# Projections of a cross-attention kernel from float32r halves to scaled float16 halves, with the key scale moved

## What is computed

```python
Q = (layernorm(x) @ Wq.T + bq).reshape(bs, sl, 16, 32)
K = (ctx @ Wk.T + bk).reshape(bs, sl, 16, 32)
V = (ctx @ Wv.T + bv).reshape(bs, sl, 16, 32)
score  = einsum('bshd,bsgd->bshg', Q, K)      # over the 16 heads of one token
weight = softmax(score)
attn   = einsum('bshg,bsgd->bshd', weight, V)
x = x + attn @ Wo.T + bo
x = x + ffn(layernorm(x))   # shared gated FFN + top 2 of 8 experts
```

## Time and profile before

| | before |
|---|---|
| median of 3 runs | 1497.16 us (1495.56 to 1502.17) |
| the profiled execution's own time | 1501.36 us |
| its span, first to last instruction | 1499.6 us |
| busy: PE, PE weight loads, DVE | 1404.5, 1070.5, 910.6 us |
| busy: ACT, POOL | 647.0, 504.6 us |
| mean granted TensorE clock | 0.979 |

### The profile page before, as it was taken

One profiled execution on the slowest core, in us unless ns is written; L12 is line 12 of the kernel. 1 busy time (PEld: TensorE's weight loads), 2 busy tenths in 40 slices (PEclk: granted clock), 3 DMA queues, 4 the chain that ended last, 5 costly groups with the idle time before them and its releaser, 6 DMA issues.

```text
span 1499.6 us, 32986 instructions
## 1 busy us (share of the span) xinstructions
PE 1404.5 (94%) x10371; PEld 1070.5 (71%) x10388; DVE 910.6 (61%) x1984; ACT 647.0 (43%) x1500; POOL 504.6 (34%) x607
## 2 busy tenths in 40 slices
PE   4899999999999998789999899999999999999997
PEld 4788888888888887557666666666666666657675
DVE  5888888888888887848764542222222222224565
ACT  6355556666666666622253433333333333332121
POOL 4444444444444442201566201111111111104554
PEclk9899999999999999799999999999999999999998
DMA  5556667666666775658655342222222222227996
GB/s 194 135 126 176 176 175 176 175 175 175 179 183 179 190 204 150 219 207 307 88 53 78 74 133 86 84 84 79 82 84 84 77 85 83 84 70 222 306 323 196
DMA packets 261893, 223.20 MB, mean 149 GB/s; under 512 B 182997, under 2 KB 191261, under 8 KB 261486
## 3 DMA queue, kind: packets, MB, share of 16 engines
q1 hardware_dynamic: 241224, 178.62, 42.6%
q0 software_dynamic: 12880, 35.47, 8.3%
q10 hardware_dynamic: 7734, 8.40, 1.9%
HBM read 129.30 MB, written 67.96 MB: 132 GB/s over the span
## 4 chain that ended last, share of the span: by engine, by line
PE 78%; DVE 8%; DMA 7%; ACT 3%; issue 2%; SPq 1%; POOL 0%; another core or an unknown queue 0%; ACTq 0%; DVEq 0%; POOLq 0%
PE psum_b L716 41%; PE psum_a L716 30%; PE psum_b L1032 2%; DMA base<-x_rows 2%; DMA base_rows<-base 2%; PE psum_a L813 2%; PE psum_b L1054 2%; ACT spread_t L1100 1%; DVE d_m L1716 1%; SPq L487 1%; DMA out_rows<-wgu_in 1%; PE psum_b L742 1%; DMA heads<-in_wk_t 1%; DVE base L1711 1%; ACT z_parts L1136 1%
## 5 line engine op out<-in xcount | busy, mean ns | idle before, releaser
L716 PE MATMUL psum_a<-wgu,zg_t 128*128 x1704 | 266.1, 313 | 1.9 <-DVE zg_t L1813 1.7
L1952 POOL TENSOR_TENSOR spread<-pr,own 128x512 f32<-128x512 f32 x128 | 136.7, 1099 | 303.2 <-DVE pr L1468 292.0
L716 PEld LDWEIGHTS psum_a<-wgu,zg_t 128*128 128x128 f16 x1704 | 165.3, 98 | 89.2 <-issue 10.1
L2026 POOL DMA_INDIRECT zg<-z_rows,gather_ix x71 | 67.2, 946 | 414.9 <-DVE gather_ix L1809 407.6
L716 PE MATMUL psum_a<-zt_in,wsgu 128*128 128x256 f16 x1536 | 177.0, 279 | 10.5 <-DMA base<-x_rows 7.5
L716 PEld LDWEIGHTS psum_a<-zt_in,wsgu 128*128 128x128 f16 x1536 | 152.1, 100 | 37.7 <-DMA base<-x_rows 9.0
L1818 DVE SCALAR_TENSOR_TENSOR silu<-psum_a,w_scale,silu 128x352 f32<-128x352 f32 x71 | 41.4, 584 | 192.0 <-ACT silu L1307 192.0
L716 PE MATMUL psum_b<-wdn,act_t 128*128 (+1 forms) x639 | 149.7, 379 | 1.6 <-DVE act_t L1825 1.6
L716 PE MATMUL psum_b<-wsdn,sh_t 128*128 128x512 f16 (+1 forms) x576 | 133.7, 386 | 16.8 <-DVE sh_t L1697 16.2
L1307 ACT ACTIVATE silu<-psum_a,w_scale 128x352 f32<-128x352 f32 x71 | 39.3, 553 | 200.8 <-PE psum_a L716 200.8
L716 PEld LDWEIGHTS psum_b<-wsdn,sh_t 128*128 128x128 f16 (+1 forms) x576 | 54.4, 99 | 90.4 <-issue 17.8
(11 more groups left out here) (245 smaller groups left out, 2510.7 us busy)
## 6 DMA issues: line engine op xcount, KB each, us to landing
expert_rows<-y_sb SPq DMA_DIRECT2D x71, 256.0 KB, 2.0
k_st<-k_parts SPq DMA_DIRECT2D x192, 64.0 KB, 2.1
q_st<-q_parts SPq DMA_DIRECT2D x180, 64.0 KB, 2.1
wgu_in<-in_wgu_t SPq DMA_DIRECT2D x8, 1408.0 KB, 17.4
x_sb<-in_x SPq DMA_DIRECT2D x16, 512.0 KB, 4.1
cx_in<-in_ctx_t SPq DMA_DIRECT2D x16, 512.0 KB, 7.0
x_res<-in_x SPq DMA_DIRECT2D x16, 512.0 KB, 5.5
value_rows<-heads SPq DMA_DIRECT2D x16, 512.0 KB, 7.0
```

What stands on the lines that cost most here:

```text
L716: return nc.tensor.matmul(o, l, r, start=start, stop=stop)
L1952: G.tensor_tensor(spread[:, u * UG:(u + 1) * UG, :].rearrange("p r (g t) -> p r g t", t=GT), pr[:, s, u * UG:(u + 1) * UG, :].unsqueeze(3) ...
L2026: pool.indirect_dma_start(out=zg[:, b, :], out_offset=None, in_=z_d[:, :], in_offset=bass.IndirectOffsetOnAxis(ap=gather_ix[:, b:b + 1], a ...
```

## The change

K, Q and V take float16 parts under power-of-two scales: 2^11 for normalised x, a scale per block for the context (`k_next`, columns 4 and 5), a scale per weight (`w_power`). V is unscaled when it is read. The sizes of `wq`, `wk`, `wv`, `xn_t`, `cx_t` halve. Since the context's scale must be known before it is split, the context block is loaded a second time, one block earlier, into `cx_w` (`load_cw`), reduced there three blocks ahead, and the seven instructions of the key scale now run behind `normalise_out`; `take_key_scale` at their old place is two instructions. POOL's `split_context` waits for it and has one more instruction over 128 x 1024. In the prologue three rounds of limits take the place of one, and the low parts of wk, wq, wv are all made by DVE. Cut to its core:

```diff
+        cx_w = sb("cx_w", [P, KC, BT], F32, early)
+        cx_t = sb("cx_t", [P, 2, KC, BT], F16, early)
+        wq, wk, wv: [P, 2, KC, D], F16;  xn_t: F16
+        LIMITS = [(0, 3), (3, 5), (5, 6)]
@@ sync, prologue
             load_w(wk_in, wk_t, wk_loaded)
+            load_cw(1)
             load_w(wq_in, wq_t, wq_loaded)
...
-            sp.wait_ge(cx_weighed, 1)
+            sp.wait_ge(cx_weighed, 2)
             load_cx(1)
+            load_cw(2)
             move_keys(-1)
             sp.wait_ge(xn_ready, 2 * SUB)
             load_x(2)
+            sp.wait_ge(cx_weighed, 3)
+            load_cw(3)
             store_values(-1)
@@ sync, body
                 if ahead:
                     store_values(i)
+                if ahead3 and ahead4:
+                    sp.wait_ge(cx_weighed, i + 4)
+                    load_cw(i + 4)
                 if ahead3:
-                    sp.wait_ge(cx_weighed, i + 3)
                     sp.wait_ge(cx_split, i + 3)
                     load_cx(i + 3)
@@ tensor, prologue
             turn_x(-1)
-            pe.wait_ge(wk_split, 1)
+            turn_limits(0)               # 3 transposes
+            pe.wait_ge(wk_split, 2)
             project_k(-1, range(KC))
-            (4 transposes of limit_rep)
+            turn_limits(1)               # 2
+            turn_limits(2)               # 1
             pe.wait_ge(wq_split, 1)
             project_q(-1, range(KC))
             pe.wait_ge(wv_split, 1)
             project_v(-1)
@@ scalar, prologue
-            weights_high(wk ...); x_out(-1); weights_high(wq ...); weights_high(wv ...)
             (two mask copies)
-            weights_high(wo, wo_in, wo_loaded, 32)
+            x_out(-1)
+            scaled_high(0, wk, ..., slice(0, KC // 2))
+            scaled_high(0, wk, ..., slice(KC // 2, KC))
+            scaled_high(1, wq, ..., slice(0, KC))
             keys_out(-1, 0); keys_out(-1, 1); queries_out(-1, 0); queries_out(-1, 1)
+            scaled_high(2, wv, ..., slice(0, KC))
             act.wait_ge(q_low, 2)
             (12 DMAs that move the queries)
+            weights_high(wo, wo_in, wo_loaded, 32)
@@ vector
+            def take_key_scale():
+                link(V.tensor_scalar(k_bound[:, 3:4], k_scale[:, 2:3], q_scale[:, 3:4], None, ALU.mult))
+                V.tensor_copy(k_scale[:, 2:10 + KC], k_next[:, 2:10 + KC]).then_inc(k_scaled, 1)
@@ vector, values_out and x_low
-                    V.tensor_tensor(v_rows[:, s], bank_ap(f"V{s}"), bv_rep[:, :], ALU.add)
+                    V.scalar_tensor_tensor(v_rows[:, s], bank, k_scale[:, 8:9], bv_rep, mult, add)
@@ vector, body
                 own_scores(i, 0, range(2))
-                next_key_scale(i - 1)
+                take_key_scale()
...
                 if behind:
                     normalise_out(i)
+                if ahead2:
+                    next_key_scale(i - 1)   # 7 instructions, then c_scaled
...
-                if ahead2:
-                    weigh_context(i + 2)
+                if ahead3:
+                    weigh_context(i + 3)    # reads cx_w
                 if ahead:
                     spread_context()
@@ vector, prologue
+            weigh_context(0)
+            dve.wait_ge(wk_loaded, 16);  largest_of(0, wk_in)
+            dve.wait_ge(bias_loaded, 64); largest_of(1, bias_col[:, 1, :])
+            weigh_context(1); max;  spread_limits(0)
+            key_scales()                     # limits_out(0), w_scaled, key scale, c_scaled
+            k_scale <- k_next
+            scaled_low(0, ...) for two halves of wk -> wk_split
             x_low(-1)
+            largest_of(3, bias), largest_of(4, wq_in); spread_limits(1)
+            query_scales()                   # limits_out(1), w_scaled
+            largest_of(5, wv_in); spread_limits(2)
+            scaled_low(1, ..., wq) -> wq_split
+            value_scales()                   # limits_out(2), w_scaled
             own, strip_sum
             low_heads K0, K1; weigh_context(2); spread_context; low_heads Q0, Q1
+            scaled_low(2, ..., wv) -> wv_split
             x_stats(1); normalise_x(1); values_out(-1); split_bias()
@@ gpsimd, split_context
+                pool.wait_ge(c_scaled, i if not isinstance(i, int) else max(i, 1))
+                link(G.tensor_scalar(cx_in[:, :, :], cx_in[:, :, :], k_next[:, 5:6], None, ALU.mult))
                 link(G.tensor_copy(cx_t[:, HI], cx_in[:, :, :]))
-                low(G, cx_t[:, LO], cx_in[:, :, :], cx_t[:, HI]).then_inc(cx_split, 1)
+                G.tensor_tensor(cx_t[:, LO], cx_in, cx_t[:, HI], ALU.subtract).then_inc(cx_split, 1)
@@ gpsimd, prologue
-            weights_low(2, wq, wq_in, wq_split)
-            weights_low(3, wv, wv_in, wv_split)
...
-            weights_low(4, wo, wo_in, wo_split)
+            weights_low(5, wo, wo_in, wo_split)
```

More of the change, by code:

```diff
@@ L193, in build @@
         bv_rep = sb("bv_rep", [P, D], F32, one)
[L194 to L196 removed]
+        limits = sb("limits", [P, 6], F32, one)
+        q_scale = sb("q_scale", [P, 5 + KC], F32, one)
+        k_bound = sb("k_bound", [P, 4], F32, one)
+        w_power = sb("w_power", [P, 8], F32, one)
+        k_next, k_scale = (sb(n, [P, 10 + KC], F32, one) for n in ("k_next", "k_scale"))
         own = sb("own", [P, GT], F32, one)
@@ L573, in load_piece, with body @@
                     sp.dma_start(weigh_in[0:FS - 5 * P, 2 * D:PIECE], wsdn_t[5 * P:FS]).then_inc(piece_loaded, 16)
-            def body(i, behind, ahead, ahead3, rows_from=None):
+            def body(i, behind, ahead, ahead3, rows_from=None, ahead4=True):
                 fetch_values(i)
@@ L895, in _, with turn_limits @@
             turn_x(-1)
-            pe.wait_ge(wk_split, 1)
+            def turn_limits(phase):
+                pe.wait_ge(limits_ready, phase + 1)
+                for n in range(*LIMITS[phase]):
+                    at = phase * BANK + (n - LIMITS[phase][0]) * P
+                    last = nc.tensor.transpose(psum_a[:, at:at + P], limit_rep[:, n, :], ident[:, :])
+                last.then_inc(limits_turned, 1)
+            turn_limits(0)
+            pe.wait_ge(wk_split, 2)
             project_k(-1, range(KC))
[L898 to L901, removed]
+            turn_limits(1)
+            turn_limits(2)
             pe.wait_ge(wq_split, 1)
@@ L1408, in weigh_context @@
                 dve.sem_inc(cx_weighed, 1)
             def spread_context():
[L1411 to L1423, removed]
+                V.tensor_copy(c_rep[:, :], k_bound[:, 2:3].broadcast_to([P, P])).then_inc(c_rep_ready, 1)
@@ new lines, in limits_out, with weight_scale @@
+            def limits_out(phase):
+                first, end = LIMITS[phase]
+                dve.wait_ge(limits_turned, phase + 1)
+                link(V.tensor_reduce(out=limits[:, first:end], in_=psum_a[:, phase * BANK:phase * BANK + (end - first) * P].rearrange("p (n c) -> p n c", c=P),
+                                     axis=X, op=ALU.max))
+            def weight_scale(n, limit):
+                power, up = (w_power[:, at:at + 1].bitcast(U32) for at in (n, 3 + n))
+                link(V.tensor_scalar(power, limits[:, limit:limit + 1].bitcast(U32), EXPONENT, None, ALU.bitwise_and))
+                link(V.tensor_scalar(power, power, float(SMALLEST << 23), None, ALU.max))
+                link(V.tensor_scalar(up, power, -1.0, float((2 * 127 + W_EXP) << 23), ALU.mult, ALU.add))
+                dve.sem_inc(w_scaled, 1)
@@ L1539, in weigh_piece, with body @@
                     V.tensor_reduce(out=seen[:, bass.ds(i, 1)], in_=weigh_in[:, 0:n], axis=X, op=ALU.max, apply_absolute_value=True).then_inc(weighed, 1)
-            def body(i, behind, ahead, ahead2, weighs=0):
+            def body(i, behind, ahead, ahead2, weighs=0, ahead3=True):
                 bound_out(i - 1)
@@ L1635, in _, with largest_of, spread_limits @@
-            V.tensor_copy(limit_rep, limits[:, :].unsqueeze(2).broadcast_to([P, 4, P])).then_inc(limits_ready, 1)
+            def largest_of(n, values):
+                mark(V.tensor_reduce(out=limits[:, n:n + 1], in_=values, axis=X, op=ALU.max, apply_absolute_value=True))
+            def spread_limits(phase):
+                first, end = LIMITS[phase]
+                own_.wait()
+                V.tensor_copy(limit_rep[:, first:end], limits[:, first:end].unsqueeze(2).broadcast_to([P, end - first, P])).then_inc(limits_ready, 1)
@@ new lines, in _ @@
+            dve.wait_ge(wk_loaded, 16)
+            largest_of(0, wk_in.rearrange("p c n -> p (c n)"))
+            dve.wait_ge(bias_loaded, 16 * 4)
+            largest_of(1, bias_col[:, 1, :])
+            own_.wait()
+            weigh_context(1)
+            link(V.tensor_tensor(limits[:, 2:3], limits[:, 2:3], k_bound[:, 2:3], ALU.max))
+            spread_limits(0)
+            key_scales()
+            V.tensor_copy(k_scale[:, 2:10 + KC], k_next[:, 2:10 + KC]).then_inc(k_scaled, 1)
+            for half in range(2):
```

(1 more changed line is left out.)

149 lines of the change are left out of this document (97 added, 52 removed).

## The result

The changed kernel takes **1517.84 us** (median of 4 runs, 1516.06 to 1520.99) against 1497.63 (1495.56 to 1502.17): a ratio of **1.0151**, interval 1.0112 to 1.0190. Its span is 1519.3 us, 19.7 more than before. The range and the sign of the prediction held. Two of its steps did not: what sets a pass, and what POOL's new instruction costs. Runs on other chips are given as a ratio to the kernel before, measured on the same chip.

A forecast was written before the change was run, and what follows sets the result against it. The passes looked bound by PE, but SP's 36.64 us loop was taken to bind. Prologue 19.4 - 1.4 - 1.2 from the passes = +16.8 us, 1514 on the median; forecast 1513, range 1501 to 1523.

The forecast's parts named there:

- The loop gives 2.6 us: Passes: total gain 2.6 us, from 1.4 of slack by pass 11 and 1.2 in passes 12 to 14.
- SP stays at 36.64 and binds: Passes: SP's queue and DMA loop keeps its 36.64 us period, so PE ends up waiting for query parts.
- DVE's 35.9: Passes: DVE's loop after the change, about 35.9 us, summed from z-to-end 8.1 and end-to-z 27.8.
- The end-to-z term: Passes, DVE from a pass's end to the second z: 27.8 us, 28.9 before.
- The z-to-end term: Passes, DVE from z to the pass's end: 8.1 us, 7.5 before, with `c_rep` ending with POOL's longer split.
- POOL's multiply, 1.1 us: POOL's added multiply over 128 x 1024 in the context split: 1.1 us, between 1.04 and 2.37.
- Matmuls: Passes, PE: 96 float16 matmuls of 256 columns save 0.9 us a pass; V nothing, bounds -0.2 to +0.2.
- Prologue: Start of the kernel: K at 25.5, Q 40.7, V 54.3, pass 0's bound at 76.6 against 56.97, +19.6 us.
- SP does not bind: Rival, passes: the engines' 35.9 us hold for 14 passes, -5.6 instead of -2.6 us; chance 0.12.
- The passes lengthen: Rival, passes: POOL's multiply at the two-operand price or SP's fetch behind the second context load, 1520 to 1528; chance 0.15.
- Float16 gives PE nothing: Rival, PE's matmuls: the 111 ns is from another tile mix, 1516; chance 0.07.
- Faster: Rival, prologue: added steps hide under existing waits, body 0 begins within 4 us of 56.97, total 1488; chance 0.06.

The follow-up runs named there:

- run 8: Kernel before with unscaled float16 tiles, POOL's parts behind z, bias split early, and DVE's expert-weight search cut to 512 columns: 1482.95 us.
- run 1: Changed kernel with DVE's search for the expert weights' scale cut to 512 columns from 1536 or 1408: ratio 1.0133.
- run 3: Changed kernel without POOL's multiply, so the context is not scaled: ratio 1.0171.
- run 4: Kernel before with the tiles of wq, wk, wv, xn_t and cx_t in float16, unscaled, same order of work: 1530.03 us, ratio 1.0195.
- run 10: Changed kernel with the prologue reordered: query weight's limits turned ahead of the first K, wv's parts made ahead of the query parts: ratio 1.0075.
- run 9: As run 8, and SP moves only two of the three key parts in the passes: 1471.62 us.
- run 5: As run 4, and in the passes POOL begins the next slab's parts only when both halves of z are written: ratio 0.9948.
- 11: As run 5, with the bias split early and POOL's second spread of a pass waiting for both halves of the next xn: ratio 0.9909.
- run 6: Kernel before with the ten instructions that split the output bias moved in front of the second slab's statistics: ratio 0.9971.

## Why the prediction was right, and where it was wrong

- **"The loop gives 2.6 us": wrong, and by the step "SP stays at 36.64 and binds".** The passes lost 1.2 us (+21.6 at the end of pass 0, +22.8 at that of pass 14). DVE's loop was put at 35.9 and is 36.65. SP's period before the change was read rightly: when DVE is relieved, SP's slack runs out and passes go to 36.5 (run 8). But in the kernel after, SP's lead was never used up. The forecast of a pass, 36.6, was right for a wrong reason, and one of the prediction's own signs of being wrong came: passes 8 to 11 took 36.51, less than SP's loop of 36.64. The second context load, put at 0, seems to cost SP 0.3 us a pass: its x loads are 36.90 apart in run 1, where it binds, and were 36.64 without that load. No run takes the load out.
- **DVE's 35.9 is 36.5 by the same two stretches, and failed in both.** The end-to-z term, 27.8, is 29.1: "-1.0 us ahead of z" did not arrive. `x_low` waits 0.82 us for ACT, as the text allowed for. The other loss I did not see: xn takes 0.88 us a half in the mean instead of 0.57 (the two groups below). All of it is in the second half, 1.37 us for 0.54, because the spread on POOL no longer waits for PE and starts under it. From the end of a pass to the second z it is 29.1 us (400.08 to about 429.2), as before (376.54 to 405.69). The z-to-end term, 8.1, is 7.4: `c_rep` was to end with POOL's subtraction, and ended with its cast. These two errors, 1.3 too little and 0.7 too much, partly cancel.

```profile
L1390 DVE TENSOR_SCALAR xn<-x_sb,mv,rstd 128x512 f32<-128x512 f32 x32 | 18.0, 565 | 3.9 <-POOL rstd L1908 3.0
```

That was the kernel before; the kernel after:

```profile
L1419 DVE TENSOR_SCALAR xn<-x_sb,mv,rstd 128x512 f32<-128x512 f32 x32 | 28.1, 877 | 4.0 <-POOL rstd L2004 3.0
```

- **POOL's multiply, 1.1 us: 2.86 to 3.91.** The upper bound, 2.37, was too low as well: here the form with one tensor and a scalar column is dearer than the form with two tensors. In the passes it hardly matters (0.15 us, run 3): POOL is then at its cast when `c_rep` is due and holds it until 435.6, where before it was at its subtraction; in the prologue it is on the path.
- **Matmuls: K and Q as said** (24 K in 2.64 us from start to start, 110 ns). V was counted at 0, bounds 0.2; it gives 5.72 - 5.34 = 0.4 us. Of the 2.0 us by which V's end moved against z in run 4, these are 0.4; the rest is its earlier start against z. A sum can be right to 0.4 us and still miss what a sooner end sets free.
- **Prologue: +19.6 said, +20.9 found.** K 25.5 (28.27), Q 40.7 (43.25), V 54.3 (56.75), bound 76.6 (77.83). K was 2.8 late: 1.4 because the scales were ready at 20.8 and not at 19.4, and 1.4 because POOL's three instructions behind them took 7.3 us (3.91, 1.04 and 2.12, and the gaps), where 6.1 had been allowed with the conflict. wk's two low halves took 3.26 instead of 2.56 beside the multiply, but ended at 24.03 and were not on the path. Q and V are 2.5 late as well, the bound 1.2. Q at the lower clock was right: 7.1 said, 7.20 found, with 0.50 granted from 42 to 46 us, behind a pause of PE. I costed the limits turned behind K, and wv's parts behind the queries, as facts of the change; run 10 shows that this order, not the work, is 13 of the 20.9 us.
- **The rivals.** "SP does not bind" was right of SP, but the passes did not come to the engines' 35.9. "The passes lengthen" named the right engine with the wrong consequence: the multiply came above its price, the passes lengthened by 0.2 to 0.3 us, not 0.6. "Float16 gives PE nothing" is out (run 9). "Faster" is out: pass 0's bound came 20.9 us late, where it needed under 5.
- **The end, and luck.** The sum gave +16.8 us; at the end of pass 14 it was +22.8. The 6 us are 2.2 up to the end of pass 0 (21.6 against 19.4) and 3.8 in passes 1 to 14, where a gain of 2.6 was said and a loss of 1.2 came. At the end of the run +19.7 was left. That difference is less than the part behind pass 14 varies, and no run tells whether it is the change's: by it the number looks closer than the working was.

The Trainium skill, "SBUF — State Buffer" (the shared port pair), says that a VectorE instruction in a two-port mode, or one with two SBUF inputs beside a GpSimd instruction that reads SBUF, shares a pair of ports with GpSimd: whichever starts first has them for its whole length, and the other blocks. For `c_rep` the trace agrees: its copy, 0.23 us alone, ends 0.1 us after POOL's cast. It shows the same in two places where I did not apply it: z at 425.23 and 426.45, whose halves ended 0.28 us after POOL's cast and its subtraction (428.51), and the second half of xn, which ended 0.28 us after POOL's first spread instruction (in the kernel after, the two starts lie within 0.04 us, too close to say which was first). Runs 5 and 11 remove these overlaps, and z goes from 1.42 to 0.54 us a half, xn from 0.84 to 0.57. For the splits of the prologue it held only in part. POOL's multiply (20.80 to 24.71) took 1.05 us over its best beside wk's first low half (20.77 to 22.05), but the second low half (21.98 to 24.03) ended 0.68 us before the multiply did; the measurement decides, and the two did not run one behind the other.

## What to carry to other kernels

Before a shorter matmul is counted, list what its end releases on the engines that share ports: here float16 alone cost 2% and one semaphore wait turned it into a gain. When several loops of nearly one length stand side by side, measure each by relieving the others; the period of the pass says which binds only when something of known size (a piece of 1408 columns for 1536) changes in one of them. In a prologue, try the small turns that a scale needs ahead of the big matmuls: here that order gave 13 us.

## What the runs showed of the hardware

- POOL multiplied 128 x 1024 float32 values by a column scalar in 2.86 us at best, cast as many in 1.04 and subtracted two tensors in 2.14.
- DVE instructions of 0.2 to 0.7 us, alone, took 2.2 to 4.9 us when POOL was in a longer instruction (0.68 alone in run 6, against 4.90); z, xn and `c_rep` ended within 0.3 us of POOL's instruction, so the price hangs on an order of start within tenths of a microsecond.
- PE's waits of 1.82 and 1.64 us at z were followed by a granted clock of 0.50 for 3.4 or 6.8 us in eight of ten passes of run 4, and by no fall in the other two; with one wait of 1.0 to 1.2 us it stayed at 1.00 in the same passes of run 5.
- K in float16 took 110 ns for 256 columns against 120 before, and V 222 ns for 512 (5.34 / 24) against 238.
